# A 512-point Hadamard product on one core: all of it on TensorE, or a 4-point part on GpSimd and a 128-point part on TensorE

## The reference

```
x  = x + ffn0(layernorm(x), weight)
ffn0: H  = hadamard(512) / sqrt(512)          # entries +1/-1, H512 = H4 (x) H128
      xh = x @ H
      scale = clip(max(|xh|, axis=-1), 1e-5) / 7
      xq = clip(round(xh / scale), -8, 7) * scale
      out = xq @ ternary(weight).T
```

## Time and profile before

| what | value |
|---|---|
| profiled execution | 2063.8 us, span 2062.1 us |
| median of three runs | 2068.04 us |
| mean granted TensorE clock | 0.928 of full speed |
| TensorE busy | 1787.1 us (87%) |
| VectorE busy | 1333.4 us (65%) |
| ScalarE busy | 997.2 us (48%) |
| GpSimd busy | 897.2 us (44%) |

### The profile page before, as it was taken

One profiled execution on the slowest core, in us unless ns is written; L12 is line 12 of the kernel. 1 busy time (PEld: TensorE's weight loads), 2 busy tenths in 40 slices (PEclk: granted clock), 3 DMA queues, 4 the chain that ended last, 5 costly groups with the idle time before them and its releaser, 6 DMA issues.

```text
span 2062.1 us, 49947 instructions
## 1 busy us (share of the span) xinstructions
PE 1787.1 (87%) x18714; PEld 1078.6 (52%) x18714; DVE 1333.4 (65%) x2518; ACT 997.2 (48%) x1858; POOL 897.2 (44%) x909
## 2 busy tenths in 40 slices
PE   4569898899988989889898899958746999999998
PEld 2335566565665756556565565635533444444443
DVE  4545787777877868778687786867586434444442
ACT  3534747566474665746657476544434222222221
POOL 1434638366382653737447374443423212222221
PEclk9679899998998999999999998969978999999999
DMA  4210202202021020210202112060232011111100
GB/s 161 98 49 27 86 12 87 71 27 97 2 96 71 27 97 1 97 70 28 96 2 97 55 43 96 2 233 1 91 128 72 1 42 41 41 41 41 41 21 21
DMA packets 48609, 124.12 MB, mean 60 GB/s; under 512 B 5644, under 2 KB 9868, under 8 KB 47384
## 3 DMA queue, kind: packets, MB, share of 16 engines
q1 hardware_dynamic: 46104, 112.64, 15.5%
q0 software_dynamic: 2304, 8.39, 1.0%
HBM read 81.17 MB, written 31.46 MB: 55 GB/s over the span
## 4 chain that ended last, share of the span: by engine, by line
PE 54%; DVE 19%; issue 11%; POOL 6%; DMA 4%; DVEq 2%; ACT 2%; SPq 1%; POOLq 0%; ACTq 0%
PE psum L1512 8%; PE psum L1502 8%; PE psum L1322 5%; PE psum L1302 5%; PE psum L1450 4%; PE psum L1303 4%; PE psum L1306 4%; POOL arena L776 3%; PE psum L1405 3%; DVE arena L1120 2%; DVE arena L1036 2%; DVEq L1037 2%; DMA arena<-in_ctx 2%; DVE psum L1130 2%; PE psum L1483 2%
## 5 line engine op out<-in xcount | busy, mean ns | idle before, releaser
L776 POOL TENSOR_TENSOR arena<-arena 128x512 f16<-128x512 f32 x512 | 565.2, 1127 | 242.3 <-ACT arena L924 240.0
L916 ACT ACTIVATE arena<-psum 128x512 f32<-128x512 f32 x512 | 307.3, 607 | 276.2 <-PE psum L1465 143.9
L924 ACT ACTIVATE arena<-arena 128x512 f16<-128x512 f32 x512 | 325.7, 642 | 6.8 <-PE psum L1485 6.3
L1302 PE MATMUL psum<-arena 128*128 128x512 f16 x672 | 262.0, 390 | 6.8 <-DVE arena L1047 6.3
L964 ACT ACTIVATE arena<-psum,arena 128x512 f32<-128x512 f32 x128 | 88.1, 688 | 361.3 <-PE psum L1502 361.3
L1303 PE MATMUL psum<-arena 128*128 128x512 f16 x672 | 259.4, 386 | 0.0
L1306 PE MATMUL psum<-arena 128*128 128x512 f16 x672 | 259.1, 386 | 0.0
L1512 PE MATMUL psum<-arena 128*128 128x512 f16 x1024 | 242.0, 378 | 8.9 <-DVE arena L1247 7.5
L1502 PE MATMUL psum<-arena 128*128 128x512 f16 x1024 | 243.0, 380 | 1.4 <-DVE arena L1235 1.4
L1483 PE MATMUL psum<-arena 128*128 128x33 f16 x2048 | 203.4, 182 | 41.6 <-POOL arena L776 39.6
L1450 PE MATMUL psum<-arena 32*128 32x256 f16 x4608 | 182.0, 293 | 62.6 <-issue 26.7
(11 more groups left out here) (117 smaller groups left out, 3255.0 us busy)
## 6 DMA issues: line engine op xcount, KB each, us to landing
arena<-x_scratch SPq DMA_DIRECT2D x48, 512.0 KB, 5.0
arena<-in_x SPq DMA_DIRECT2D x32, 512.0 KB, 5.8
arena<-in_L_ffn_W SPq DMA_DIRECT2D x16, 1024.0 KB, 5.2
arena<-arena SPq DMA_DIRECT2D x16, 512.0 KB, 5.7
x_scratch<-arena POOLq DMA_DIRECT2D x16, 512.0 KB, 3.9
x_scratch<-arena SPq DMA_DIRECT2D x16, 512.0 KB, 3.4
out<-arena SPq DMA_DIRECT2D x16, 512.0 KB, 3.2
arena<-in_ctx SPq DMA_DIRECT2D x16, 384.0 KB, 7.4
```

The lines of the kernel that those rows point to most:

```text
L776: gp.tensor_tensor(pl[l][:, h % NP, :], pf[l][:, h % NF, :], ph[l][:, h % NP, :], ALU.subtract).then_inc(p_lo[l].sem, 1)
L916: sc.activation(pf[l][:, h % NF, :], bank(u.bank), ACT.Exp, scale=SCALE / (QS * QS) if l == 0 else SCALE).then_inc(read[u.bank], 1)
L924: sc.activation(ph[l][:, h % NP, :], pf[l][:, h % NF, :], ACT.Copy).then_inc(p_hi[l].sem, 1)
L1302: te.matmul(out, x_hi, w[:, 0, c, :], start=(c == 0), stop=False)
```

## The change

The 512-point product is taken apart as H4 (x) H128. The 4-point part is done by GpSimd on the normalised tile in fp32, ahead of the turn: two instructions write sums and differences of neighbouring chunks into a scratch (`sums`, which lies in `ph_raw[0]`), two more write sums and differences of its halves back into the tile. Each is 128 partitions by 256 elements, and each waits for the one before; the last one signals `mixed`. `turn_ffn` on TensorE waits for `mixed` instead of `xnF_ready`. The 128-point part stays on TensorE: the same number of matmuls, each with 128 columns instead of 512, each chunk to its own quarter of the bank. The constant shrinks from 128x512 to 128x128.

```diff
-        had = take(2 * P).bitcast(F16)
+        had = take(P // 2).bitcast(F16)
...
+        sums = [ph_raw[0][:, k * D:(k + 1) * D].rearrange("p (a c n) -> p a c n", a=2, c=2) for k in range(NT)]
...
+        mixed = Signal(sem("mixed"), 2)
...
-        had_rows = [had[:, 0:P].unsqueeze(1).to_broadcast([P, 4, P]),
-                    had[:, 0:2 * P].unsqueeze(1).to_broadcast([P, 2, 2 * P]),
-                    had[:, 0:2 * P].rearrange("p (a n) -> p a n", a=2).unsqueeze(2).to_broadcast([P, 2, 2, P]),
-                    had]
...
+            def mix(out, src, n, op):
+                x = src.rearrange("p (a c n) -> p a c n", a=n, c=2)
+                return gp.tensor_tensor(out, x[:, :, 0], x[:, :, 1], op)
...
+                    elif kind == "normalise_ffn":
+                        k = at[0]
+                        pool.wait_ge(xnF_ready.sem, xnF_ready.at(b, k + 1))
+                        chain(mix(sums[k][:, :, 0], attn[0][:, k, :], 2, ALU.add))
+                        chain(mix(sums[k][:, :, 1], attn[0][:, k, :], 2, ALU.subtract))
+                        x = attn[0][:, k, :].rearrange("p (a c n) -> p a (c n)", a=2, c=2)
+                        y = sums[k].rearrange("p a c n -> p a (c n)")
+                        chain(gp.tensor_tensor(x[:, 0], y[:, 0], y[:, 1], ALU.add))
+                        gp.tensor_tensor(x[:, 1], y[:, 0], y[:, 1], ALU.subtract).then_inc(mixed.sem, 1)
...
                     elif kind == "turn_ffn":
-                        pe.wait_ge(xnF_ready.sem, xnF_ready.at(b, k + 1))
+                        pe.wait_ge(mixed.sem, mixed.at(b, k + 1))
                         turn(use["xf", 0, k], attn[0][:, k, :], DC)
...
-                                mm = te.matmul(bank(u.bank), oT[0][:, s, c, k * P:(k + 1) * P], had_rows[c],
-                                               start=(c + s == 0), stop=(c + s == DC))
+                                mm = te.matmul(bank(u.bank)[:, c * P:(c + 1) * P], oT[0][:, s, c, k * P:(k + 1) * P], had,
+                                               start=(c + s == 0), stop=(s == 1), skip_group_check=True)
...
-    return np.concatenate([h, -h, -h, h], axis=1).astype(np.float16)
+    return h.astype(np.float16)
```

## The result

The changed kernel takes 2144.83 us, the median of four runs (2144.61 to 2147.42), against 2069.32 beside it: a ratio of 1.0369, 95% interval 1.0351 to 1.0387. It is slower by 75.5 us. The profiled execution is 2144.62 with a span of 2142.9, 80.8 above the span before. The forecast was 2130 in a range of 2090 to 2165. The mechanism held, but one of its terms, the price of the low clock, was half of what it measured.

The account below looks back on a forecast made before the run. TensorE was taken to bound the kernel (54% of the chain), with GpSimd having time to spare. Fourteen passes at 2.95 + 1.2 us late gave 58, plus 4 for first and last: 62, so 2130 us on the median, range 2090 to 2165.

Parts of the forecast that it names:

- The product at 0.058 per matmul: TensorE's product: 128-column matmuls start 0.058 us apart at full clock, against 0.216 for 512 columns; 2.5 us saved per batch.
- The mixing at 0.72 and 3.1 a tile: GpSimd's four chained adds and subtracts: 0.72 us each, 3.1 us per tile with the waits, bounds 2.3 and 5.3.
- The places: Queue positions around the product: turn 0 4.05 us late, turn 1 5.85 late, small pair and next normalises behind the mixing.
- The projection 2.95 late without the clock: TensorE's projection behind the product starts at 1065.3 instead of 1062.37, 2.95 us late per pass, saving already included.
- The clock, 1.2 a pass: TensorE behind the gap drops to 1.2 GHz: 2.0 us lost, 1.2 more per pass after cover, bounds 0 and 3.
- of which its wait of 0.75 covers part: TensorE's new 0.75 us wait before the projection, on a VectorE held up by GpSimd, absorbs part of the 2.0 lost.
- the 62 of the sum: Whole kernel: 14 x (2.95 + 1.2) = 58 us plus 4 for first and last pass, 62 us slower.
- the 4: First and last pass together: 4 us slower, from at most +2.6 in the first and +1 in the last.
- Rival (a), the clock holds: TensorE stays at 2.4 GHz behind the gap: 45 us slower, 2113 us; chance 0.18 with its cheaper mixing.
- Rival (b), a long low clock: TensorE's clock stays low for long behind the gap: 88 us slower, 2156 us; chance 0.13 with the dearer mixing.
- Rival (c), faster below 1.6 us a tile: GpSimd's mixing under about 1.6 us a tile keeps the pass; at half that, 41 us saved, 2027; chance 0.03.
- Rival (d), weights set the pace at 128 columns: TensorE's product: each 128-column matmul takes 0.10 us because it brings its weights, 9 us more, 2139; chance 0.04.

## Why the prediction was right, and what was mis-sized

- *The product at 0.058 per matmul:* 0.056 at full clock. The 81 ns of the Trainium skill (TensorE: Matmul & The Clock Gate, "Back-to-back issue gap") isn't seen here.
- *The mixing at 0.72 and 3.1 a tile:* 0.73 per instruction. Tile 0 took 3.3 (1111.24 to 1114.57): its first instruction, which runs beside VectorE's normalise, took 0.9; tile 1 took 3.15. GpSimd is 95.3 busier in all, for the forecast's 95.
- *The places:* turn 0 4.05 late, turn 1 5.85 late, the small pair and the next layer's normalise behind the mixing. Measured from the end of the heads, turn 0 is 4.2 late and turn 1 6.1, 0.2 and 0.25 more than forecast, which is the mixing's extra.
- *The projection 2.95 late without the clock:* 3.30 with idle matmuls in the gap. The difference is mostly the mixing.
- *The clock, 1.2 a pass:* 2.26, **the mis-sized term**. The loss itself was near the forecast's 2.0: from 1117.80 on, to the next start each, turn 1 takes 0.91 for 0.50 with the clock up, the projection 2.56 for 1.29, product 0 0.85 for 0.45, which makes 2.1. What failed is "of which its wait of 0.75 covers part". The wait exists (0.73), but it isn't on a VectorE that was held up by GpSimd: it is the copy and split behind TensorE's own turns, which the wide product 1 used to cover. It moves with the turns and covers nothing: it is 0.73 with the low clock and 0.73 without. Between the profiled executions there are 80.8 us for the 62 of the sum: 14 x (2.26 - 1.2) = 14.8 is the clock and 14 x (3.30 - 2.95) = 4.9 mostly the mixing; the first and the last pass gave 3.3 for the 4.
- *Rival (a), the clock holds:* out; its 2113 is what the run with idle matmuls measured, 2110.85.
- *Rival (b), a long low clock:* out, product 1 is at full clock in every full pass.
- *Rival (c), faster below 1.6 us a tile:* the turning point was right for the stretch (8.12 at half the mixing with the clock up). Its price was not: by the text 41 us come through with free mixing, and 17 did.
- *Rival (d), weights set the pace at 128 columns:* out by the 0.056 of product 1.

## What to carry to other kernels

Before work is moved to an engine with spare time, look at where in its queue the spare time lies, and which engine stands idle for the hand-over: here 3 us a tile on an engine busy for 55% of a pass cost more than the matmuls saved. A gap of some us on TensorE can have a second price behind it, the half clock, which was 34 of 75 us here; idle matmuls in the gap show how much. And where the work that is shortened covers another engine's copy or split, part of the saving comes back as a wait: price the saving by a run with the saving alone.

## What the hardware showed beside this

VectorE's fp32 sum of 128x256 (L1170 in the run with the mixing on VectorE) took 1.19 us while GpSimd ran its subtraction, and 0.43 alone, 2.8 times. Product 0's pitch with the wide product varied from 0.216 to 0.366 from pass to pass, while the changed kernel's was 0.093 to 0.107. TensorE's pause without a releaser in the scores stood behind the 45th matmul in the kernel before, in the changed kernel and with half of the mixing, in 11 of the 13 passes each; the 13 idle matmuls of the half-mixing run moved it behind the 8th in those, and its last stretch was 1.7 us longer.
